# Cross-attention and expert FFN on one core: the context split as it lies and transposed by DMA one pair ahead

## The reference, cut to what matters

```python
x = x + xattn(layernorm(x), ctx, ctx, Wq, bq, Wk, bk, Wv, bv)   # x, ctx: 16 x 256 x 256, f32
x = x + ffn(layernorm(x), Wg, W1, b1, W2, b2)                   # 8 experts, hidden 1024

def xattn(query, key, value, ...):
    Q = query @ Wq + bq;  K = key @ Wk + bk;  V = value @ Wv + bv
    return softmax(Q @ K.T / sqrt(256)) @ V

def ffn(x, ...):               # expert choice: each expert takes its 1024 best rows of 4096
    G, I = top_k(sigmoid(x @ Wg).T, 1024)
    out = (gelu(x[I] @ W1 + b1) @ W2 + b2) * G
    return zeros.at[I].add(out)
```

## Time and profile before

| | us |
|---|---|
| median of 3 runs | 547.64 (547.56 to 548.38) |
| profiled execution, its own time | 549.17 |
| profiled execution, span | 547.4 |
| PE busy | 491.1 (90% of the span) |
| DVE busy | 332.0 (61%) |
| ACT busy | 307.8 (56%) |
| POOL busy | 293.2 (54%) |
| mean granted TensorE clock | 0.944 of full speed |

### The profile page before, as it was taken

The page is one execution under the profiler, slowest core; times in us unless marked ns, Lnnn a source line. Parts: engine busy times, 40 slices in busy tenths (PEclk is TensorE's granted clock), DMA queues, the critical chain, the costliest instruction groups (busy, mean ns, idle before and its releaser), DMA issues.

```text
span 547.4 us, 10408 instructions
## 1 busy us (share of the span) xinstructions
PE 491.1 (90%) x3671; PEld 351.6 (64%) x3671; DVE 332.0 (61%) x739; ACT 307.8 (56%) x562; POOL 293.2 (54%) x436
## 2 busy tenths in 40 slices
PE   4999999998523299999999999999999999999995
PEld 3777777777411245864874884794685586486484
DVE  7477777876588847547538538546645654733720
ACT  3666666654534059249439519727826925935921
POOL 5736998893600416734653671671672763555055
PEclk9999999998655589999999999999999999999998
DMA  7312555545195155943862771771782593484024
GB/s 237 107 46 69 153 147 134 137 131 150 38 275 157 41 130 172 171 72 127 141 121 76 156 144 27 200 149 19 195 162 29 152 180 55 136 126 49 0 31 50
DMA packets 91929, 64.19 MB, mean 117 GB/s; under 512 B 53044, under 2 KB 87800, under 8 KB 91896
## 3 DMA queue, kind: packets, MB, share of 16 engines
q1 hardware_dynamic: 79248, 46.42, 31.1%
q0 software_dynamic: 12288, 17.05, 18.8%
q10 hardware_dynamic: 360, 0.30, 0.2%
HBM read 35.83 MB, written 16.91 MB: 96 GB/s over the span
## 4 chain that ended last, share of the span: by engine, by line
PE 59%; issue 6%; DVE 5%; POOL 4%; DMA 2%; SPq 2%; ACT 1%; POOLq 0%; DVEq 0%; ACTq 0%
PE bank L1026 54%; PE bank L1257 3%; POOL out L460 2%; DVE junk L794 2%; SPq L266 2%; POOL xrow L387 1%; DMA out<-yo,ids_s 1%; DMA rows_d<-xrow 1%; POOL ex L447 1%; DVE thr L815 1%; PE bank L1233 1%; DMA ex<-rows_d,ids 1%; DMA yo<-xrow 0%; DVE oneh L907 0%; POOL xrow L379 0%
## 5 line engine op out<-in xcount | busy, mean ns | idle before, releaser
L1026 PE MATMUL bank<-w2h,xres 128*128 128x256 f16 x1024 | 169.0, 273 | 0.0
L1026 PE MATMUL bank<-exT,w1h 128*128 128x512 f16 x512 | 153.3, 381 | 0.6 <-DVE exT L1012 0.6
L1026 PE MATMUL bank<-w2l,xres 128*128 128x256 f16 x512 | 139.7, 273 | 0.0
L967 DVE TENSOR_TENSOR xres<-g,xres 128x512 f16<-128x512 f32 x128 | 87.6, 690 | 60.4 <-ACT xres L598 60.4
L460 POOL DMA_INDIRECT out<-yo,ids_s x64 | 101.0, 1577 | 25.6 <-issue 24.9
L1026 PEld LDWEIGHTS bank<-w2h,xres 128*128 128x128 f16 x1024 | 100.1, 98 | 12.5
L594 ACT ACTIVATE g<-bank,b1e 128x512 f32<-128x512 f32 x128 | 88.0, 688 | 25.4 <-PE bank L1026 20.3
L611 ACT ACTIVATE yo<-yt,ge 128x256 f32<-128x256 f32 x64 | 32.5, 508 | 119.5 <-DVE yt L981 119.5
L1026 PE MATMUL bank<-exT,w1l 128*128 128x512 f16 x256 | 97.7, 381 | 0.0
L1026 PEld LDWEIGHTS bank<-exT,w1h 128*128 128x128 f16 x512 | 49.8, 98 | 59.5 <-issue 1.4
L598 ACT ACTIVATE xres<-bank,b1e 128x512 f16<-128x512 f32 x128 | 87.2, 681 | 0.0
(11 more groups left out here) (215 smaller groups left out, 779.7 us busy)
## 6 DMA issues: line engine op xcount, KB each, us to landing
w1r<-in_L_ffn_W SPq DMA_DIRECT2D x8, 1024.0 KB, 6.6
w2r<-in_L_ffn_W SPq DMA_DIRECT2D x8, 1024.0 KB, 5.3
ctx<-in_ctx SPq DMA_DIRECT2D x8, 512.0 KB, 5.0
xres<-in_x SPq DMA_DIRECT2D x8, 512.0 KB, 5.9
rows_d<-xrow SPq DMA_DIRECT2D x8, 512.0 KB, 3.5
out<-xres SPq DMA_DIRECT2D x4, 1024.0 KB, 9.1
b_bc<-in_L_ffn_b SPq DMA_DIRECT2D x8, 128.0 KB, 4.5
ex<-rows_d,ids POOLq DMA_INDIRECT x64, 3.8
```

The source lines that it names most:

```text
L967: dve.tensor_tensor(hid[1][:, f, h * 512:(h + 1) * 512], g32[:, u % 2, :], hid[0][:, f, h * 512:(h + 1) * 512], ALU.subtract).then_inc(s[" ...
L1026: last = pe.matmul(out, lhs(a, c), rhs(b, c), start=i == 0, stop=i == len(terms) - 1)
```

## The change

The context is no longer transposed on PE, except for pair 0. ACT and DVE split it from `ctx` as it lies into `crow` (row-major, high and low part side by side), and SP issues 4 DMA transposes (128 x 512 half-precision each) that write both parts of `cT`. There are two `cT` now, the second and `crow` in the memory of `oneh`, which is used only after phase A. Splitting and transposing are done for pair n+2 in step n, where the PE path worked on pair n+1. Pair 1 is split in step 0, and SP transposes it ahead of its loop.

```diff
-        cT = [sb(f"cT{i}", [P, DC, PAIR], F16) for i in "hl"]
+        cT0 = sb("cT0", [P, 2 * DC, PAIR], F16)
...
+        crow = spare[:, 0:2 * TP * D].rearrange("p (t a d) -> p t a d", t=TP, a=2)
+        cT = [cT0, spare[:, 2 * TP * D:4 * TP * D].rearrange("p (c k) -> p c k", c=2 * DC)]
...
# SP
+            def context_T(m):
+
+                sp.wait_ge(s["c_lo"], m + 1)
+                if m >= 2:
+                    sp.wait_ge(s["v_mm"], m - 1)
+                for t in range(TP):
+                    sp.dma_start_transpose(cT[m % 2][:, :, t * P:(t + 1) * P], crow[:, t].rearrange("p a d -> p (a d)")).then_inc(C_T[m % 2], 16)
+
             def body(n, k):
                 if n + 2 < NP:
-                    sp.wait_ge(s["c_tr"], n + 1)
+                    if n:
+                        sp.wait_ge(s["c_lo"], n + 1)
+                    else:
+                        sp.wait_ge(s["c_tr"], 1)
                     sp.dma_start(ctx[:, n % 2], cv[:, tiles(n + 2), :]).then_inc(LD_C[n % 2], 16)
                     sp.wait_ge(s["ln1_st"], 2 * (n + 1))
                     sp.dma_start(xres[:, tiles(n + 2), :], xv[:, tiles(n + 2), :]).then_inc(LD_X[n % 2], 16)
+                if n + 2 < NP:
+                    context_T(n + 2)
...
+            context_T(1)
             phase_a(body)
# ACT
+            def split_context(m):
+
+                act.wait_ge(LD_C[m % 2], landed(m))
+                if m >= 2:
+                    act.wait_ge(C_T[(m - 1) % 2], 16 * TP * ((m - 1) // 2 + (m - 1) % 2))
+                act.activation(crow[:, :, 0, :], ctx[:, m % 2], ACT.Copy, scale=XS).then_inc(s["c_hi"], 1)
...
                 if k == 0:
+                    split_context(1)
...
-                if runs(n, k, -1):
-                    hi(cT[0][:], B_[:], "c_tr", "c_hi", n + 2, scale=XS)
+                if n + 2 < NP:
+                    split_context(n + 2)
# DVE
+                if k == 0:
+                    lo(crow[:, :, 1, :], ctx[:, 1], crow[:, :, 0, :], "c_hi", 2, "c_lo", XS)
...
-                if runs(n, k, -1):
-                    lo(cT[1][:], B_[:], cT[0][:], "c_hi", n + 2, "c_lo", XS)
+                if n + 2 < NP:
+                    lo(crow[:, :, 1, :], ctx[:, n % 2], crow[:, :, 0, :], "c_hi", n + 3, "c_lo", XS)
# PE
-                pe.wait_ge(s["c_lo"], n + 1)
-                if n == 0:
+                if n:
+                    pe.wait_ge(C_T[n % 2], 16 * TP * (n // 2 + n % 2))
+                else:
+                    pe.wait_ge(s["c_lo"], 1)
...
-            def transpose_ctx(n):
-
-                pe.wait_ge(LD_C[(n + 1) % 2], landed(n + 1))
-                if n:
-                    pe.wait_ge(s["p_lo"], 2 * n)
-                transposes(B_, ctx[:, (n + 1) % 2], 0, TP).then_inc(s["c_tr"], 1)
...
-                if runs(n, k, -1):
-                    transpose_ctx(n)
```

More of the change, by code:

```diff
@@ L158, in build @@
         inhi = sb("inhi", [P, NT, KT])
+        spare = oneh[:].rearrange("p a t -> p (a t)").bitcast(F16)
+        crow = spare[:, 0:2 * TP * D].rearrange("p (t a d) -> p t a d", t=TP, a=2)
+        cT = [cT0, spare[:, 2 * TP * D:4 * TP * D].rearrange("p (c k) -> p c k", c=2 * DC)]
         val = sb("val", [P, NT, 2, KT], BF16)
@@ L195, in build @@
             ln1_st ln1_var ln1_rstd ln1_mr ln1_nmr xn_rdy xbv wg_hi_s wg_lo_s
-            x_tr x_hi x_lo c_tr c_hi c_lo g_mm g_hi g_lo v_mm v_hi v_lo
+            x_tr x_hi x_lo c_tr c_hi c_lo c_t0 c_t1 g_mm g_hi g_lo v_mm v_hi v_lo
             s_mm s_max s_nb s_exp s_ri p_tr p_hi p_lo o_mm o_ev
@@ L216, in runs @@
             return 0 <= k - shift < NP
+        C_T = s["c_t0"], s["c_t1"]
         LD_X, LD_C = (s["ld_x0"], s["ld_x1"]), (s["ld_c0"], s["ld_c1"])
@@ L524, in _ @@
             hi(w_hi[:], w_raw[:, 2], "ld_wv", "w_hi_s", 16, scale=AS)
-            hi(cT[0][:], C_[:], "c_tr", "c_hi", 1, scale=XS)
+            hi(cT0[:, 0:DC], C_[:], "c_tr", "c_hi", 1, scale=XS)
             hi(m_w[0][:].rearrange("p c d -> p (c d)"), A_[:, 0, :], "m_mm", "m_hi", 1, scale=1.0 / AS)
@@ L675, in _ @@
                 stats(0, st1, "ln1", h)
-            lo(cT[1][:], C_[:], cT[0][:], "c_hi", 1, "c_lo", XS)
+            lo(cT0[:, DC:], C_[:], cT0[:, 0:DC], "c_hi", 1, "c_lo", XS)
             lo(m_w[1][:].rearrange("p c d -> p (c d)"), A_[:, 0, :], m_w[0][:].rearrange("p c d -> p (c d)"), "m_hi", 1, "m_lo", 1.0 / AS)
@@ L1088, in project_g @@
                     pairs(A_[:, e, :], lambda a, d: m_w[a][:, d, e * P:(e + 1) * P],
-                          lambda b, d: cT[b][:, d, :], DC).then_inc(s["g_mm"], 1)
+                          lambda b, d: cT[n % 2][:, DC * b + d, :], DC).then_inc(s["g_mm"], 1)
             def transpose_p(n):
@@ L1102, in project_v @@
                 for t in range(TP):
-                    last = pairs(D_[:, t // 2, (t % 2) * D:(t % 2 + 1) * D], lambda a, d: cT[a][:, d, t * P:(t + 1) * P],
+                    last = pairs(D_[:, t // 2, (t % 2) * D:(t % 2 + 1) * D], lambda a, d: cT[n % 2][:, DC * a + d, t * P:(t + 1) * P],
                                  lambda b, d: wsp[b][:, d, :], DC)
```

## The result

| | before | after |
|---|---|---|
| median, us | 548.01 (547.56 to 549.37) | 586.07 (583.65 to 587.34) |
| ratio to before, 95% interval | 1 | 1.0685 (1.0642 to 1.0728) |
| profiled execution, span | 547.4 | 585.4 |
| mean granted TensorE clock | 0.944 | 0.918 |

The kernel became 6.9% slower. The forecast was 579.0, with a range of 567 to 590; the narrower own range of 574 to 586 was just missed. As before, the starts M(n) of `row_max(n)` tell the story; the gate is the activation behind the last logits, which ends phase A.

What follows compares the result with a forecast made beforehand. The prediction took the loop of DVE and ACT as the bound, with SP's queue order deciding the cost. Terms 10.3 + 1.3 + 16.3 + 4.3 - 0.8 = 31.4 on a median of 547.64 gave 579.0 us, range 567 to 590 (own 574 to 586).

Steps and rivals of the forecast that it cites:

- PE transposes worth nothing: Phase A: removing PE's context transposes, 6.1 us of PE, gains 0, since the DVE and ACT loop hides them.
- Step 0: `row_max(0)` starts at 38.4 instead of 28.08, held up by context 2's load behind context 1's transposes: +10.3 us.
- Step 1: PE idles 11 us ahead of `project_g(1)`, then starts at 1.2 GHz, making `g`'s second half late: +1.3 us.
- Steps 3 to 5: Period 20.0 instead of 14.56 us, from load and router chains behind SP's transposes plus a lowered clock: +16.3 us.
- Splitting from SBUF: Context splits on DVE and ACT cost 1.2 and 1.0 us, as before: 0, bounds -0.1 to +0.2 a step.
- Step 6: No context split, but `router(3)` still waits for transposes queued behind context 7's; 18.9 us: +4.3.
- The end: At `router(5)`, the earlier 0.81 us idle for `xrow`'s transposes is hidden because PE comes later: -0.8 us.
- Nothing behind it: Behind `router(5)`, nothing changes: search and experts wait for no context.
- the unlowered clock: Rival: PE's clock isn't lowered in pauses, steps 3 to 5 take 18.6 us each; 571.8 us, chance 0.20.
- PE as the bound: Rival: PE limits the steps and the loads keep up; -6.1 us, 541.5; chance of faster 0.04.
- the hidden case: Rival: all added work is hidden, SP's issues fitting into the step; 547.6 us, chance 0.04.
- Slower transposes: Rival: eight DMA transposes in a row slow towards 2.37 us each; up to +35 more, chance 0.10.

Runs made afterwards that it cites:

- experiment 10: The kernel before the change with its 8 context transposes on PE run twice in each step; 547.75 us, ratio 1.0019.
- Experiment 3: The changed kernel with context 1 split ahead of its first step and pair 2's loads issued ahead of context 1's transposes; 578.28 us, ratio 1.0562.
- experiment 1: The changed kernel with each pair's context and x loads issued ahead of the transposes that held them up; 582.34 us, ratio 1.0637.
- experiment 2: The changed kernel with the transposes of `xrow` and its store put ahead of the context's transposes; 567.65 us, ratio 1.0363.
- experiment 4: The changed kernel with 48 unused matmuls on PE before `router`, shortening its pause; 584.6 us, ratio 1.0672.
- experiment 5: The changed kernel with DVE's low part of the context computed from PSUM instead of `ctx`; 581.7 us, ratio 1.0628.
- experiment 8: As kernel 6, with DVE's low split moved behind the statistics of the next pair, where DVE waits for ACT; 552.12 us, ratio 1.0073.
- experiment 9: As kernel 6, with two `crow`, loads a further pair ahead and the low split in DVE's next gap; 554.39 us, ratio 1.0126.
- kernel 6: The changed kernel with loads first, `xrow`'s transposes and store ahead of the context's, and context 1 split ahead of the first step; 556.62 us, ratio 1.0167.

## Why the prediction was right, and where it was off

- *PE transposes worth nothing*: right. Shown from the other side by experiment 10; that removing them gains nothing is read from the same loop.
- *Step 0, +10.3*: measured +9.7. The load landed 3.9 us after its issue, not 4.6. Experiment 3 gives 6.7 of it back.
- *Step 1, +1.3*: measured +1.3, by the predicted means: PE idle 10.26, granted clock 0.63 from 30 to 40 and 0.72 from 40 to 45.
- *Step 2, 0*: measured +0.8. The low split took 1.99 us there, 0.8 over its price.
- *Steps 3 to 5, +16.3*: measured +21.6, the term that was mis-sized. The mechanism is the one named, by experiments 1, 2 and 4. (The landing of 5.1 in the load's chain is that of the earlier trace rows, not of rows 7 as the prediction has it.) The 5.3 missing fall on two pieces. From `row_max` to `router` it is 12.47, 12.78 and 12.58 instead of 11.8, +2.4: the two groups of transposes take 11.0 to 11.3 us instead of 10.4, since in each pair of groups one takes 5.8 to 6.1: the term "I take 1.27, the same shape in the same place" was too small as well. And from `router` to `row_max` it is 9.1 to 9.2 instead of 8.2, +2.85, of which 2.35 are the low split. The clock, put at 1.7 in each of these steps, took 2.5, 2.0 and 1.4 by experiment 4's rows.
- So the step of the prediction that failed is "Splitting from SBUF ... 0, bounds -0.1 to +0.2 a step". It took its price from the earlier trace rows, in the first 20 us, with nothing beside it. In place it is 0.2 to 1.4 over, for as long as POOL's sum runs beside it (last section). I had not asked what POOL reads at that moment.
- *Step 6, +4.3*: measured +3.6 (18.20). It has no low split, and its wait for the rows was 5.06.
- *The end, -0.8*: measured -0.2. I had PE come too late to wait for the last rows. It waited more, 2.27 instead of 0.81: step 7 had become 1.15 us shorter (10.53 against 11.68), for the pause of the earlier trace rows was gone, and `router(5)` stayed where its rows let it.
- *Nothing behind it*: measured +1.6 by the second load of W2, of which 1.1 is left at the end. The search is not longer (36.47 from the gate to PE's next work in both). PE came out of it at 1.2 GHz in both, but kept it longer afterwards. The kernel after, and the stretches of the kernel before that lie 37 us earlier:

```profile
233.00:235.00 2.00, 2.00 (x25) 1.45 (x24) 0.78 (x2) 0.85 (x2) 0.00 (x0) 0.50 0.15 31
235.00:237.00 2.00, 2.00 (x6) 0.65 (x5) 0.00 (x0) 0.15 (x1) 0.00 (x0) 0.50 0.51 102
237.00:241.00 4.00, 4.00 (x19) 1.82 (x18) 2.32 (x4) 3.61 (x6) 0.00 (x0) 0.95 0.53 110
```

```profile
196.00:198.00 2.00, 2.00 (x27) 1.62 (x26) 0.78 (x2) 0.92 (x2) 0.00 (x0) 1.00 0.13 28
198.00:200.00 2.00, 2.00 (x11) 0.88 (x9) 0.00 (x0) 1.27 (x2) 0.00 (x0) 1.00 0.53 105
```

It is the same difference as in experiment 5, and perhaps also why runs of the kernel after spread over 3.7 us; that was not tested.

Of the rivals, the unlowered clock falls by the rows above, PE as the bound by experiment 10, the hidden case and that of the first steps by the periods. Slower transposes were a small part: 5.8 to 6.1 us for some groups, far from the 9.5 of that rival. The order of the lists is 29 of the 38 us. What stays with that order is 1.7%, or 0.7% with the split moved; no kernel here beats the one before.

What stays open: why one group of transposes in a step takes up to 1 us more, why PE started its matmuls at half the rate ahead of step 0 in some executions, and what would move the rows of `router(5)`, which take back what the steps gain; no run changed that chain alone.

## What to carry to other kernels

Work taken off an engine is worth only what that engine held up; doubling it is a cheap way to ask. Before a DMA is added to a queue that issues in order, write down what stands behind it there and what waits for that: here the loads of the next pair and the router's rows stood behind four transposes and their wait, and the order of the lists was three quarters of the loss. A pause that a queue puts into PE is paid twice, once as the pause and again as 1.2 GHz behind it (2.5 us in one step here). But a gain in the steps is one only if the last wait of the stage moves too: kernels 4, 8 and 9 lost theirs at `router(5)`. Price an operation that moves from PSUM to SBUF beside what POOL reads at that time, and POOL's own work beside it.

## What the runs showed of the hardware

- **A split with two SBUF inputs stands still while POOL reads SBUF.** It has two, as has POOL's sum (L389, L393), which takes 2.35 us. Where the sum starts first, the split's duration follows the overlap to 0.01 us (overlap: end of the sum less start of the split):

| kernel, split at | overlap | split took | less overlap |
|---|---|---|---|
| after, 88.93 | 0.36 | 1.44 | 1.08 |
| after, 110.34 | 0.89 | 1.97 | 1.08 |
| after, 131.47 | 1.49 | 2.57 | 1.08 |
| experiment 8, 71.10 | 0.67 | 1.75 | 1.08 |
| experiment 8, 55.12 | 1.73 | 2.82 | 1.09 |
| experiment 8, 84.58 | 2.10 | 3.19 | 1.09 |

  The 1.08 are 0.13 less than a split with nothing beside it; no run shows why. The other way round POOL stands still. In step 2 of the kernel after, POOL and DVE:

```profile
65.56 2.13 POOL L405 TENSOR_TENSOR xrow<-xn,xrow 128x1024 f16<-128x1024 f32 x1 [0.15 <-POOL xrow L397]
67.65 3.33 POOL L389 TENSOR_TENSOR xres<-xres,bv_bc 128x1024 f32<-128x1024 f32 x1
```

```profile
66.78 1.99 DVE L663 SCALAR_TENSOR_TENSOR oneh<-ctx,oneh 128x1024 f16<-128x1024 f32 x1
```

  The split waits out the operation at 65.56, and the sum at 67.65 is 0.98 longer, for the 1.12 us until the split ends. By the Trainium skill ("SBUF — State Buffer", "Who interferes with whom") a VectorE instruction with two SBUF inputs contends with a GpSimd instruction that reads SBUF, the shared ports are an exclusive lock, and issue order decides who is blocked; with at most one SBUF input, outside the modes that use both ports, it does not contend. The trace agrees: the rows above for the lock, POOL's 5.92 instead of 4.85 us in experiment 9 for a POOL operation with one tile to read, and experiment 5, whose split reads PSUM, for the last, with 1.20 to 1.23 throughout.
- **DMA transposes.** All instructions of L260 in the kernel after (issue in ns; landing in us):

```profile
L260 SPq DMA_TRANSPOSE oneh<-oneh x16: 1196/1268/2262, 26.4 to 137.9; - x16
L260 SPq DMA_TRANSPOSE cT<-oneh x12: 1195/1267/1988, 37.9 to 116.2; - x12
...
DMA to landing us min/median/max: 2.4/2.5/4.3
```

  The median is that of the earlier trace rows; single ones take 1 us more. The Trainium skill ("VectorE: DVE Perf Modes", "The three transpose paths") has 1309 ns for one 128x128 on this path; here 1.27 us went over four such blocks.
- **The clock's fall and return** vary behind like pauses. Behind 6.08 and 5.76 us of idle PE ran at 1.2 GHz for some 3 us in one kernel and some 6 in another. Behind 2.12 and 2.16 us, ahead of step 1, the granted clock was 0.53 for 3.2 us in kernel 3 and 1.00 in kernel 6.
